# Three transposes of a local-attention layer passed through DRAM, and a layer's weights loaded at other points

## The reference, cut to what matters

```python
q, k, v = split(x @ Wqkv)                       # 16 heads of 64
q, k = l2norm(q) * qs, l2norm(k) * ksc
q = q * cos * scale + rotate_half(q) * sin * scale
k = k * cos / scale + rotate_half(k) * sin / scale
# windows of 32 queries see their own and the previous 32 keys
attn = softmax(mask(einsum('bhwie,bhwje->bhwij', q, k2) * 8))
out = einsum('bhwij,bhwje->bhwie', attn, v2)
x = shift(out @ Wo + x); x = feed_forward(x) + x    # in outline
```

## Time and profile before

| | |
|---|---|
| Median of 3 runs | 3499.77 us (3498.44 to 3503.96) |
| The profiled execution's own time | 3499.11 us |
| Span of its trace | 3497.3 us |
| Mean granted TensorE clock | 0.951 of full speed |
| Busy share of the span | PE 91%, DVE 83%, ACT 65%, POOL 52% |
| DMA engines, mean busy share | 46.4% (398 MB moved) |
| From one L1062 to the next | 61.60 us in most steps, 65 to 69 us in two steps of each layer change |

### The profile page before, as it was taken

One profiled execution on the slowest core, in us unless ns is written; L12 is line 12 of the kernel. 1 busy time (PEld: TensorE's weight loads), 2 busy tenths in 40 slices (PEclk: granted clock), 3 DMA queues, 4 the chain that ended last, 5 costly groups with the idle time before them and its releaser, 6 DMA issues. The chain is left out here.

```text
span 3497.3 us, 71552 instructions
## 1 busy us (share of the span) xinstructions
PE 3165.8 (91%) x25368; PEld 1997.4 (57%) x25560; DVE 2895.0 (83%) x2723; ACT 2273.7 (65%) x3693; POOL 1808.8 (52%) x823
## 2 busy tenths in 40 slices
PE   5769999999999999999956899999999999999996
PEld 3536655655656666666533566666666566566563
DVE  4559988988988988988924899898898898898994
ACT  1147776766766776777712677677777777777773
POOL 5535555555555555555500555555565555555551
PEclk8789999999999999999977999999999999999998
DMA  5444454454454554554411445445445445445442
GB/s 183 160 116 101 111 135 107 116 127 109 115 130 107 122 124 104 122 127 108 99 34 66 101 104 140 114 97 144 109 103 141 110 105 140 105 111 137 111 111 60
DMA packets 273778, 399.12 MB, mean 114 GB/s; under 512 B 75836, under 2 KB 104248, under 8 KB 273720
## 3 DMA queue, kind: packets, MB, share of 16 engines
q1 hardware_dynamic: 273720, 398.48, 46.4%
HBM read 66.34 MB, written 19.92 MB: 25 GB/s over the span
## 5 line engine op out<-in xcount | busy, mean ns | idle before, releaser
L927 POOL TENSOR_TENSOR f_w<-f_w,f_ab 128x1024 f32<-128x1024 f32 x192 | 554.9, 2890 | 568.2 <-DVE f_w L964 568.2
L923 POOL TENSOR_TENSOR f_u<-f_u 128x512 f32<-128x512 f32 x384 | 582.0, 1530 | 464.0 <-ACT f_u L809 464.0
L932 POOL TENSOR_TENSOR f_ab<-f_w,f_rn 128x1024 f32<-128x1024 f32 x192 | 588.3, 3064 | 321.8 <-DVE f_rn L974 310.7
L809 ACT ACTIVATE f_u<-ps 128x512 f32<-128x512 f32 x768 | 466.6, 608 | 162.9 <-PE ps L628 84.9
L810 ACT ACTIVATE f_ab<-ps,f_pa 128x512 f32<-128x512 f32 x768 | 540.8, 704 | 1.2
L964 DVE TENSOR_TENSOR f_w<-f_ab,f_tan 128x1024 f32<-128x1024 f32 x384 | 498.9, 1340 | 4.6 <-POOL f_ab L932 4.6
L626 PE MATMUL ps<-f_xh,f_wh 128*128 128x512 f32 x768 | 384.2, 500 | 118.3 <-ACT f_ab L810 100.6
L684 PE MATMUL ps<-f_tb,f_v 128*64 128x160 f32 (+1 forms) x6144 | 446.9, 299 | 18.4 <-DMA f_tb<-f_pt 17.1
L684 PEld LDWEIGHTS ps<-f_tb,f_v 128*64 128x64 f32 x6144 | 400.2, 139 | 107.7 <-issue 105.0
L663 PEld LDWEIGHTS ps<-f_kb,f_qb 128*32 128x32 f32 x12288 | 351.2, 117 | 161.4 <-issue 128.3
L821 ACT ACTIVATE ps<-ps 128x512 f32<-128x512 f32 x384 | 204.6, 574 | 359.2 <-PE ps L645 359.2
(11 more groups left out here) (169 smaller groups left out, 5034.2 us busy)
## 6 DMA issues: line engine op xcount, KB each, us to landing
f_kb<-f_ab SPq DMA_DIRECT2D x1536, 64.0 KB, 2.0
f_qb<-f_ab SPq DMA_DIRECT2D x768, 128.0 KB, 2.4
f_tb<-f_pt SPq DMA_DIRECT2D x1344, 64.0 KB, 2.0
f_wh<-split_w SPq DMA_DIRECT2D x48, 384.0 KB, 3.3
f_wl<-split_w SPq DMA_DIRECT2D x48, 384.0 KB, 3.5
a_w_raw<-wqkv SPq DMA_DIRECT2D x24, 384.0 KB, 4.0
split_w<-a_w_hi SPq DMA_DIRECT2D x24, 384.0 KB, 2.3
split_w<-a_w_lo SPq DMA_DIRECT2D x24, 384.0 KB, 2.8
```

What stands on the lines that cost most here:

```text
L809: nc.scalar.activation(u[:, i, :], bank("qk", g, i), ACT.Square).then_inc(sq_done.sem, 1)
L923: nc.gpsimd.tensor_tensor(u[:, 2 * i + 1, :], u[:, 2 * i, :], u[:, 2 * i + 1, :], ALU.add).then_inc(sq_sum[i].sem, 1)
L927: nc.gpsimd.tensor_tensor(w[:, 0:2, :], w[:, 0:2, :], ab[:, k % 2, 0:2, :], ALU.add).then_inc(q_sum.sem, 1)
L932: nc.gpsimd.tensor_tensor(ab[:, k % 2, 0:2, :], w[:, 0:2, :], rn[:, 0:1, :].broadcast_to([128, 2, N]), ALU.mult).then_inc(rope_q.sem, 1)
```

## The change

- `keys(g)` and `queries(g)` become `keys_and_queries(g)`: one write of the keys' half of `ab` to a DRAM buffer (`k_out`, 512 KB), one of the queries' half (`q_out`, 512 KB), a wait for `k_out`, two reads into `kb` (`k_in`, 256 KB each), a wait for `q_out`, one read into `qb` (`q_in`, 512 KB). 5 DMAs in place of 12.
- `weights(g)` becomes one write of `pt` to DRAM (`t_out`, 512 KB), a wait for it, and 5 reads into `tb` (`t_in`). 6 DMAs in place of 8.
- `evacuate` (ACT) now waits for `k_out` and `q_out` of quad `g - 2`; DVE's turn into `pt` waits for `t_out`; `scores` and `values` wait for the reads.
- `load_qkv` of quads 2 and 3 moves from behind `weights(2)` to between `keys_and_queries(3)` and `weights(2)`.
- `load_ff` moves from the end of the new layer's first step to its second step, between `weights(-1)` and `keys_and_queries(1)`, and out of the prologue. The inner loop is unrolled: the outer loop's body is now four steps.
- `next_tokens` takes over the wait on `x2` that stood inside `queries(0)`; it waits for an event long past.

```diff
-                        def keys(g):
+                        def keys_and_queries(g):
+                            by_row = turned_rows[g % 2].rearrange("w p h (d a) n -> w (p h d) a n", a=2)
                             sp.wait_ge(s_ready.sem, now.count(s_ready, g - 1))
                             sp.wait_ge(rope_k.sem, now.count(rope_k, g))
-                            for h in range(HQ):
-                                rows = slice(32 * h, 32 * h + 32)
-                                for a in range(2):
-                                    to = 64 * a + 32 * (h % 2)
-                                    sp.dma_start(kb[to:to + 32, h // 2, h % 2, PAD:], ab[rows, g % 2, 2 + a, :]).then_inc(k_dma.sem, 16)
-                        def queries(g):
+                            sp.dma_start(by_row[1], ab[:, g % 2, 2:4, :]).then_inc(k_out.sem, 16)
                             sp.wait_ge(rope_q.sem, now.count(rope_q, g))
-                            for pair in range(2):
-                                if pair and g == 0:
-                                    sp.wait_ge(x2.sem, now.count(x2, -3))
-                                for a in range(2):
-                                    sp.dma_start(qb[64 * a:64 * a + 64, pair, :], ab[64 * pair:64 * pair + 64, g % 2, a, :]).then_inc(q_dma.sem, 16)
+                            sp.dma_start(by_row[0], ab[:, g % 2, 0:2, :]).then_inc(q_out.sem, 16)
+                            sp.wait_ge(k_out.sem, now.count(k_out, g))
+                            for h in range(2):
+                                sp.dma_start(kb[64 * h:64 * h + 64, :, h, PAD:], turned_rows[g % 2, 1, :, h].rearrange("p r n -> r p n")).then_inc(k_in.sem, 16)
+                            sp.wait_ge(q_out.sem, now.count(q_out, g))
+                            sp.dma_start(qb[:, :, :], turned_rows[g % 2, 0].rearrange("p h r n -> (h r) p n")).then_inc(q_in.sem, 16)
...
                             sp.wait_ge(p_tr.sem, now.count(p_tr, g))
+                            passed = turned_weights[g % 2]
+                            sp.dma_start(passed, pt[:, :].rearrange("p (b n) -> p b n", b=2)).then_inc(t_out.sem, 16)
+                            sp.wait_ge(t_out.sem, now.count(t_out, g))
                             for r in range(4):
-                                sp.dma_start(tb[rows, r], ptb[rows, 1]).then_inc(t_dma.sem, 16)
-                                if r:
-                                    sp.dma_start(tb[32 * r - 32:32 * r, r], ptb[rows, 0]).then_inc(t_dma.sem, 16)
+                                own = passed[32 * r:32 * r + 32, 1]
+                                if r < 3:
+                                    both = bass.AP(tensor=own.tensor, offset=own.offset, ap=[[1024, 32], [32 * 1024 - 512, 2], [1, 512]])
+                                    sp.dma_start(tb[32 * r:32 * r + 32, r:r + 2].rearrange("p r n k -> p r (n k)"), both).then_inc(t_in.sem, 16)
                                 else:
-                                    sp.dma_start(tb[96:128, 4, 0:12], ptb[rows, 0, 4:16]).then_inc(t_dma.sem, 16)
+                                    sp.dma_start(tb[96:128, 3].rearrange("p n k -> p (n k)"), own).then_inc(t_in.sem, 16)
+                                    sp.dma_start(tb[96:128, 4, 0:12].rearrange("p n k -> p (n k)"), passed[0:32, 0, 4 * WIN:]).then_inc(t_in.sem, 16)
...
                         if prev:
                             weights(-1)
+                        if hidden_layer is not None:
+                            sp.wait_ge(x2.sem, now.count(x2, -2))
+                            load_ff(hidden_layer)
                         if cur:
-                            keys(1)
-                            queries(1)
+                            keys_and_queries(1)
                             weights(0)
...
-                            keys(3)
-                            queries(3)
-                            weights(2)
+                            keys_and_queries(3)
                             if next_layer is not None:
                                 sp.wait_ge(v_ready.sem, now.count(v_ready, 2 * TILES - 1))
                                 load_qkv(layer_rows, range(2, QUADS))
-                            if new_layer is not None:
-                                sp.wait_ge(x2.sem, now.count(x2, -1))
-                                load_ff(new_layer)
+                            weights(2)
...
                     with sp.Fori(1, DEPTH) as at:
-                        later_sequences(FIRST - B + at * B, B - 1)
+                        step(FIRST - 3 + at * B, True, True, hidden_layer=at - 1)
+                        step(FIRST - 2 + at * B, True, True)
                         step(FIRST - 1 + at * B, True, True, next_layer=at)
                         step(FIRST + at * B, True, True, new_layer=at)
...
-                                act.wait_ge(k_dma.sem, now.count(k_dma, g - 2))
-                                act.wait_ge(q_dma.sem, now.count(q_dma, g - 2))
+                                act.wait_ge(k_out.sem, now.count(k_out, g - 2))
+                                act.wait_ge(q_out.sem, now.count(q_out, g - 2))
...
-                            dve.wait_ge(t_dma.sem, now.count(t_dma, g - 1))
+                            dve.wait_ge(t_out.sem, now.count(t_out, g - 1))
```

More of the change, by code:

```diff
@@ L384, in build_hybrid @@
         gain, rope_q, rope_k = per_quad("gain"), per_quad("rope_q", ahead=1), per_quad("rope_k", ahead=1)
-        k_dma, q_dma = per_quad("k_dma", 32 * HQ, ahead=2), per_quad("q_dma", 64, ahead=2)
+        k_out, q_out = per_quad("k_out", 16, ahead=2), per_quad("q_out", 16, ahead=2)
+        k_in, q_in = per_quad("k_in", 32), per_quad("q_in", 16)
         s_ready = per_quad("s_ready", ahead=2)
@@ L388, in build_hybrid @@
         p_sum, p_inv, p_norm = per_quad("p_sum"), per_quad("p_inv"), per_quad("p_norm")
-        p_tr, t_dma = per_quad("p_tr", ahead=2), per_quad("t_dma", 32 * HQ, ahead=1)
+        p_tr, t_out, t_in = per_quad("p_tr", ahead=2), per_quad("t_out", 16, ahead=1), per_quad("t_in", 80)
         o_ready = [per_quad(f"o_ready{i}", ahead=3) for i in range(2)]
@@ L499, in _, with step @@
                     load_out(0)
-                    load_ff(0)
-                    def step(s, prev, cur, new_layer=None, next_layer=None):
+                    def step(s, prev, cur, hidden_layer=None, next_layer=None, new_layer=None):
                         now = Steps(sp, s + 1, SP_USES)
@@ L549, in step @@
                         if cur:
-                            keys(0)
-                            queries(0)
+                            keys_and_queries(0)
                             next_tokens()
@@ L563, in step @@
                                 load_qkv(layer_rows, range(1))
-                            keys(2)
-                            queries(2)
+                            keys_and_queries(2)
                             if next_layer is not None:
@@ L578, in step @@
                                 load_qkv(layer_rows, range(2, QUADS))
-                            if new_layer is not None:
-                                sp.wait_ge(x2.sem, now.count(x2, -1))
-                                load_ff(new_layer)
-                    def later_sequences(first, end):
-                        with sp.Fori(1, end) as b:
-                            step(first + b, True, True)
+                            weights(2)
                     sp.wait_ge(zeroed, 2)
@@ L654, in scores @@
                         def scores(g):
-                            pe.wait_ge(q_dma.sem, now.count(q_dma, g))
-                            pe.wait_ge(k_dma.sem, now.count(k_dma, g))
+                            pe.wait_ge(q_in.sem, now.count(q_in, g))
+                            pe.wait_ge(k_in.sem, now.count(k_in, g))
                             for tile in range(TILES):
@@ L674, in values @@
                             pe.wait_ge(v_read.sem, now.count(v_read, TILES * (g // 2) + TILES - 1))
-                            pe.wait_ge(t_dma.sem, now.count(t_dma, g))
+                            pe.wait_ge(t_in.sem, now.count(t_in, g))
                             pe.wait_ge(gain.sem, now.count(gain, at))
```

26 lines of the change are left out of this document (15 added, 11 removed).

## The result

The changed kernel takes 3622.53 us (median of 4 runs, 3610.46 to 3636.77) where the kernel before takes 3499.82 (4 runs, 3498.44 to 3503.96): ratio 1.0348, interval 1.0331 to 1.0365. The forecast was 3446 with 3408 to 3490 as its range. The change made the kernel 123 us slower, on the side that was given 0.09. The profiled execution took 3616.15 us, its span is 3614.4.

The account below looks back on a forecast made before the run. PE's own work bounds ordinary steps; SP's queue lengthens two steps per layer change. Profiled 3499.1 - 49.8 (D) - 8.8 (C) + 4.6 (keys and queries) = 3445, the median 0.7 above: 3446 us, range 3408 to 3490.

Parts of the forecast that it names:

- C: First kind of long step at layer changes, ten in all: 4.5 us over ordinary before, forecast 3.6, -8.8 in all.
- D: Second kind of long step at layer changes, ten in all: load_ff hidden, step becomes ordinary, -49.8 us.
- A: The step after D among a layer's four; an ordinary step, forecast at 61.6 to 61.8 us.
- Price of one leg: One 512 KB DMA to or from DRAM: write 2.65 us (2.3 to 3.2), read 3.3 (3.0 to 3.7).
- Keys and queries, 0.1 us a step: Quad 1's q_in lands 0.35 us late, nearly all taken up at the mask: 0.1 a step, 4.6 in all.
- Rival 3: Steadily loaded rings land each leg 0.9 us or more later; quad 1's scores 1.8 net late, 3524 us; chance 0.09.
- the share stays near 0.56, no bound: Load on the DMA engines: twice the bytes, far from twice the time, a share near 0.56, no bound.
- B: The step after A, holding the loads of quads 0 and 1; forecast as ordinary, those loads costing nothing.
- Weights: Quad -1's t_out and five reads take 6.7 to 7.2 us where 7.6 are there: hidden.
- ACT's wait: ab is free 2.7 us after rope_q instead of 4.2; PE does not feel it in ordinary steps, no gain.
- SP's queue: Issue time per quad falls from 12.4 to about 10.3 us; waits inside the queue delay nothing due in ordinary steps.
- Rival 4: SP's waits inside its queue make it late: 0.5 us a step over the forecast, 3469 us; chance 0.06.

Follow-up runs that it names:

- e6: e5 with SP's loop written out in full, so no jump back; 3412.9 us, ratio 0.9747 to the kernel before.
- e1: Changed kernel with all transposes direct from SBUF to SBUF, keeping only the new load points and unrolled loop; 3479.7 us, 0.9942 of the kernel before.
- e5: e1 with load_qkv of quads 2 and 3 moved ahead of quad 3's keys; 3441.9 us, ratio 0.9837 to the kernel before.
- e4: Changed kernel with the key reads issued ahead of the wait on rope_q and the query write; 3997.2 us, ratio 1.1421 to the kernel before.
- e7: Changed kernel with one of the two key reads left out; 3526.7 us, ratio 1.0082 to the kernel before.
- e2: Changed kernel with weights direct, only queries and keys through DRAM; 3500.2 us, ratio 0.9988 to the kernel before.
- e12: e6 with the weights alone passing through DRAM; 3407.9 us, ratio 0.9728 to the kernel before.
- e3: Changed kernel with queries and keys direct, only weights through DRAM; 3521.9 us, ratio 1.0059 to the kernel before.
- e10: Changed kernel with the two key reads of 64 partitions replaced by one of 128, same bytes; 3577.1 us, ratio 1.0224 to the kernel before.
- e8: Changed kernel with load_qkv of quads 2 and 3 put back behind weights(2); 3614.7 us, ratio 1.0328 to the kernel before.

## Why the prediction was wrong, point by point

**What bounds the kernel, the long steps.** Right. e6 shows that the place of the loads and the jump were all of C's and D's excess: 92 us against the kernel before on its own chip, from these alone.

**D, -49.8.** Half right. `load_ff` is hidden and D is ordinary but for 0.7 us (64.3 against A's 63.6), so the jump is indeed covered by the two-leg chain, in which `rope_q` decides and not the keys. But with A itself at 63.6, D gave 23.1 us and not 49.8. With direct transfers the D steps that have the jump, eight of the ten, take 3.4 (e1) to 4.0 us (e5) more than 61.6: the cover was the slower chain, not the load's place.

**Price of one leg.** The write, 2.65, was right for a write alone: `k_out` lands in 2.7, `q_out` in 2.65 in the passage shown, but in 3.0 in an A step, with the key reads right behind it. The read, 3.3 with 3.7 as its upper end, was wrong in its place: it came below 3.7 once, at 3.65. `q_in`'s landing in the changed kernel, all 192:

```profile
DMA to landing us min/median/max: 3.6/5.1/6.5
```

The price was taken from a read with nothing before it and given to one with 512 KB of keys before it and, in quads 1 and 3 (in C quad 1 alone), 512 KB of weights behind it. For a read with neither it was nearly right: 3.5 in e4. The Trainium skill (DMA: Bandwidth & Descriptors, section Anatomy of one DMA) has a fit, for DMAs issued by GpSimd, by which either leg is 3.2 us, an estimate: too much for this write (2.65), too little for this read (3.5 alone, 5.1 at the median).

**Keys and queries, 0.1 us a step: the step that failed.** The prediction put it as "the key reads are issued in its shadow". Issued, yes; but their data are not moved in that shadow, and nothing was charged for what SP issues around the two legs. In an A step the chain of quad 1 is 7.5 us and not 6.1, and PE starts the scores 1.9 late instead of 0.35. Of the 1.4 us over the forecast, 0.35 are the write's (3.0) and 1.1 the read's (4.4). Of the read's 1.1, 0.2 are its own (3.5 alone), 0.65 go with `t_out` behind it and 0.2 with the keys ahead of it (e4, without keys ahead: 4.2). In quad 3, and in quad 1 of D, the keys cost it more: 5.0 in quad 3, 4.2 with half of them (e7) and 4.1 with none (e4). Rival 3 named the place and the threshold (a chain of 7.3), but looked for it in a steady load that makes every leg longer by 0.9; it is the neighbours on the queue, and the read pays most of it. e2 isolates the term (1.6 us in A), e7 shrinks it to 0.9, e12 removes it. That "the share stays near 0.56, no bound" failed with it: 0.60 is an average, and the burst behind `rope_q` runs at 0.93.

**B, not foreseen: 4.9 us a step.** The prediction said that those loads cost nothing, from the earlier trace rows. That holds for direct transfers (e1) and for e3. With both passages quad 0's load stands ahead of quad 2's `k_out` and `q_out`, which land 4.4 and 5.3 us after their issue, and quad 1's load ahead of quad 1's `t_out`, which lands in 6.1 (medians of ten). PE waits 2.4 us for quad 2's queries, which were never late in A. An absence of cost was carried over from a chain with slack to one without.

**C, 3.6 over ordinary.** Right mechanism, wrong size: 9.3 over 61.6. `t_out` lands 14.1 after the cut and not 12.3, PE waits 4.3 to 4.7 and not 2.5, PE is busy 2.8 longer at the lower clock, for which 1.4 stood, and 2.0 are A's loss over again.

**Weights, ACT's wait, SP's queue.** Weights hidden: right (e3 in A and B, e12 everywhere), though `t_out` lands in 3.0 at the median in e12 and in 5.1 in the changed kernel, where `q_in` is right ahead of it. ACT's wait for `ab` gone without a gain: right. Rival 4, SP's waits inside the queue, costs nothing that shows in A, but e4 shows how close it is.

The sum with measured terms: D -23.1, C +48.2, A +19.9, B +48.5, and 23.6 outside these forty steps: 117.1.

The packet records show how little of this is waiting in line. In quad 1 of A the key reads' 256 packets have all started 1.3 us after `q_in` is issued, where the first packet of a `q_in` with nothing ahead starts 1.0 after its issue (e4). The rest is `q_in`'s own packets, spread over a longer time.

What stays open: why the keys lengthen the read in one quad and hardly in another. No run moves `t_out` away from `q_in` in quad 1, so what that would give back in A is not measured. Nor is it shown why the same A step takes 63.6 in one kernel and 64.7 in another.

## What to carry to other kernels

A transfer's price read where nothing stands beside it is a lower end: for a chain that decides a step, list what is issued on the same queue ahead of it while its own legs run, and right behind it as well. Here the write behind cost the read as much as the keys before it, or more. "Issued in the shadow of a wait" is time of the queue that issues and says nothing of the rings. A load that costs nothing beside a chain with 1.5 us to spare has to be priced anew once the chain is two legs long; here the gain lay in the loads' place and the jump alone, 2.5% with no change to the transfers (e6).

## What the runs showed of the hardware

- A 512 KB write to DRAM lands 2.65 us after its issue with nothing ahead. A read of the same size lands in 3.5 with nothing ahead or behind (e4), 5.1 at the median of the changed kernel.
- The same read lands in 3.85 us when loads are issued 0.6 us behind it, and in 5.0 when a 512 KB write is issued 0.5 us behind it (C steps of the changed kernel and of e8, quad 3).
- Two reads of 256 KB into 64 partitions each hold up the next transfer more than one of 512 KB into 128: 5.1 against 4.5 us for the query read behind them (e10). In the packet records of the A passages the first 128 packets of the key reads take 84 ns each, the next 128 some 150 to 160, and the queries' last 128 again 84; a 4096-byte write packet takes 159 ns, and in the kernel before a 2048-byte packet from SBUF to SBUF 152 ns.
- Rows of 4096 in place of 2048 bytes did not make the query read faster (5.3 against 5.1).
- A jump back of SP's outer loop, over a body of four steps, takes 2.7 us of its queue: the gap is 2.9 with it and 0.3 without (e5), and a D step without it takes 61.6 us.
